# Dense products of a tick between the score and the transposes, in TensorE's order of work

## What is computed

```python
h = layernorm(x, gamma1, beta1)                      # layer 0
Q, K, V = h @ Wq + bq, h @ Wk + bk, h @ Wv + bv      # 16 heads of 16
attn = softmax(where(causal, Q K^T / 4, -inf))
x1 = x + (attn V) @ Wo + bo
x2 = x1 + gelu(layernorm(x1, ...) @ W1 + b1) @ W2 + b2
x  = x + gate * (x2 - x)
x  = layernorm(up(expert(gelu(down(x)))) + x)        # layer 1, expert of each sample
x  = layernorm(gelu(x @ Wi[e] + bi) @ Wo[e] + bo + x) # layer 2, expert of each sample
x  = layernorm(x) * (1 + scale) + shift              # layer 3
scores = Q K^T / 4 + attention_bias                  # (4, 16, 512, 512), masked
x = x + (softmax(scores) V) @ Wo + bo
x = x + gelu2(layernorm(x) * g2 + beta2 @ W1 + b1) @ W2 + b2
```

## Time and profile before

| | |
|---|---|
| three runs, median (lowest to highest) | 1131.92 us (1128.73 to 1132.33) |
| the profiled execution: its own time | 1131.03 us |
| its span, first to last instruction | 1128.9 us |
| PE busy | 997.0 us, 88% |
| DVE busy | 682.5 us, 60% |
| ACT busy | 685.0 us, 61% |
| POOL busy | 281.0 us, 25% |
| mean granted clock of PE, share of full speed | 0.982 |

### The profile page before, as it was taken

How to read it: one execution, slowest core, us unless ns; L and a number is a source line. 1 busy time by engine, 2 the same in 40 slices (tenths; PEclk the granted TensorE clock), 3 DMA queues, 4 the chain that set the end, 5 groups by cost and what they waited for, 6 DMA issues and landing times.

```text
span 1128.9 us, 22058 instructions
## 1 busy us (share of the span) xinstructions
PE 997.0 (88%) x7746; PEld 662.0 (59%) x7834; DVE 682.5 (60%) x1748; ACT 685.0 (61%) x1582; POOL 281.0 (25%) x473
## 2 busy tenths in 40 slices
PE   4878889898989899998889898899898999899868
PEld 2445556556546566566647466566575657657645
DVE  5668773645855747845772666746639754764740
ACT  3457565573765665776664746666657674675721
POOL 7310020000310640630120200730903370180010
PEclk9889999899999999999999999999999999999989
DMA  5879424206252454854625119667385486935400
GB/s 161 231 166 206 76 75 102 49 11 140 38 139 76 91 179 132 192 200 149 139 75 124 66 62 192 213 173 197 126 203 186 150 199 235 238 119 201 154 1 19
DMA packets 118351, 154.78 MB, mean 137 GB/s; under 512 B 12956, under 2 KB 80924, under 8 KB 118244
## 3 DMA queue, kind: packets, MB, share of 16 engines
q1 hardware_dynamic: 113636, 147.04, 48.8%
q0 software_dynamic: 1936, 3.97, 1.3%
q10 hardware_dynamic: 2672, 2.36, 0.6%
HBM read 134.47 MB, written 18.88 MB: 136 GB/s over the span
## 4 chain that ended last, share of the span: by engine, by line
PE 57%; ACT 16%; DVE 15%; issue 11%; DMA 0%; POOL 0%; DVEq 0%; ACTq 0%; POOLq 0%
PE bank L1384 15%; PE bank L1373 9%; PE bank L1480 8%; PE bank L1494 6%; PE bank L1335 6%; PE bank L1459 4%; ACT gT L933 3%; ACT bias L886 3%; DVE mrow L1216 3%; DVE bias L1225 3%; PE bank L1349 2%; PE bank L1359 2%; PE bank L1463 2%; ACT pT L894 2%; ACT L933 2%
## 5 line engine op out<-in xcount | busy, mean ns | idle before, releaser
L886 ACT ACTIVATE bias<-bias,mrow 128x512 f32<-128x512 f32 x256 | 184.1, 719 | 186.2 <-DVE mrow L1225 184.4
L1225 DVE CUSTOM_DVE_ANT_0 bias<-bank,bias 128x512 f32<-128x512 f32 x256 | 175.0, 687 | 199.1 <-PE bank L1459 88.0
L883 ACT ACTIVATE prob<-bank,mrow 128x128 f32<-128x128 f32 (+3 forms) x256 | 134.8, 527 | 191.7 <-DVE mrow L1216 189.7
L1216 DVE TENSOR_REDUCE mrow<-bank 128x1 f32<-128x128 f32 (+3 forms) x256 | 124.3, 487 | 172.4 <-PE bank L1465 171.0
L823 POOL TENSOR_TENSOR norm_rows_t<-norm_rows_t,minus_half 128x4 f32<-128x4 f32 x22 | 22.6, 1026 | 664.5 <-DVE norm_rows_t L1099 664.5
L1480 PE MATMUL bank<-ident,bias 128*128 128x128 f32 x1024 | 156.3, 275 | 33.4 <-ACT pT L894 24.3
L1480 PEld LDWEIGHTS bank<-ident,bias 128*128 128x128 f32 x1024 | 121.4, 141 | 106.7 <-ACT bias L886 53.5
L1373 PE MATMUL bank<-hT,w 128*128 128x512 f32 x384 | 181.2, 602 | 1.6 <-ACT hT L910 0.9
L1384 PE MATMUL bank<-w,gT 128*128 128x256 f32 x768 | 174.3, 381 | 0.0
L1459 PE MATMUL bank<-ks,qs 128*128 128x512 bf16 (+3 forms) x425 | 144.0, 339 | 30.3 <-ACT prob L883 28.2
L1233 DVE COPY pT<-bank 128x512 f32<-128x512 f32 (+3 forms) x263 | 150.9, 574 | 5.9 <-PE bank L1480 5.3
(11 more groups left out here) (165 smaller groups left out, 1128.0 us busy)
## 6 DMA issues: line engine op xcount, KB each, us to landing
bias<-in_fside_Bx16xSxS SPq DMA_DIRECT2D x128, 512.0 KB, 4.4
w<-in_L_cond_W SPq DMA_DIRECT2D x16, 1024.0 KB, 5.5
qs<-q_parts SPq DMA_DIRECT2D x30, 384.0 KB, 10.4
ks<-k_parts SPq DMA_DIRECT2D x30, 384.0 KB, 11.7
q_parts<-parts SPq DMA_DIRECT2D x80, 128.0 KB
k_parts<-parts SPq DMA_DIRECT2D x48, 128.0 KB
w<-in_L_cond_Wi SPq DMA_DIRECT2D x4, 1024.0 KB, 5.0
w<-in_L_cond_Wo SPq DMA_DIRECT2D x4, 1024.0 KB, 5.8
```

Source lines behind the costliest of these rows:

```text
L883: act.activation(prob_of(U), score_bank[U % 2][:, 0:n], ACT.Exp, bias=mrow[:, U % ROW_RING:U % ROW_RING + 1], accum_out=rsum[:, U % ROW_RI ...
L886: act.activation(prob_of(U), prob_of(U), ACT.Exp, scale=-1.0, bias=mrow[:, U % ROW_RING:U % ROW_RING + 1], accum_out=rsum[:, U % ROW_RING: ...
L1216: v.tensor_reduce(m, score_bank[U % 2][:, 0:n], AX_X, ALU.max, negate=True).then_inc(max_done, 1)
L1225: v.tensor_tensor_reduce(out=prob_of(U), in0=score_bank[U % 2][:], in1=prob_of(U), scale=-1.0, scalar=3e38, op0=ALU.add, op1=ALU.min, accu ...
```

## The change

In each tick, PE's dense steps now stand directly behind `scores(U)`, ahead of `turn(U - 2)`, `values` and `spread_sums`. Before, they stood behind all of these. No instruction is added or taken away, and no other engine's order changes.

```diff
                 if 0 <= U < ALL_UNITS:
                     scores(U)
+                for step, args in steps.get(U, []):
+                    do[step](*args)
                 V = U - TURN_LAG
                 if 0 <= V < ALL_UNITS:
                     turn(V)
@@
                 V = U - SPREAD_AT
                 if 0 <= V < ALL_UNITS and V % BATCH == 0:
                     spread_sums(V // BATCH)
-                for step, args in steps.get(U, []):
-                    do[step](*args)
```

## The result

The changed kernel takes **1140.23 us** (median of 5 runs, 1136.48 to 1143.42), the kernel before 1131.92 (5 runs, 1128.73 to 1132.42): ratio 1.0071, 95% interval 1.0051 to 1.0092. It is slower by 8.3 us, above the forecast's 1130 and above its range. The profiled execution of the changed kernel took 1136.62 us with a span of 1134.7, against 1131.03 and 1128.9: the two traces differ by only 5.6 us.

The account below looks back on a forecast made before the run. PE, busy 88% of the span, was taken as the bound, its waits all that order can win. Gains 15.6, losses 11.6 and 4.4, and 1.2 from sooner results gave 0.8 us won: 1130 us (1126 to 1134).

Parts of the forecast that it names:

- first `hidden`: First `hidden` of a feed-forward layer, 11 places beside attentions: product runs while the transpose would wait, 5.4 us won.
- `project`: First projection beside an attention: some places lose a transpose or wait about 0.5 us, one wins; 1.0 us lost.
- What bounds the kernel; the rule for gains and losses: PE busy 88% of the span; ready dense steps win the transposes' waits, waiting ones lose transposes and values put behind.
- `turn_tokens`, `turn_expert`, `up`: Steps waiting for operands lose 6.1, 2.9 and 1.6 us; two turns whose transposes waited win 1.0 us.
- Later causal `hidden` and `ff_out`: Causal dense products directly behind a score: taken as costing nothing, with 0.02 us either way per tick.
- The copy ahead of the maximum: VectorE's copy starts the maximum 0.26 us later in the mean; 45 waits hang on it, 4.4 us lost.
- Later biased `hidden`, `qk`, `down`: Fifth and ninth ticks of biased layers win 4.9 us, places beside `qk` 2.6, beside `down` 1.7.
- The waits of L1459 for probabilities stay: PE's scores waiting for probabilities from ScalarE: the change cannot move these waits, which stay near 28 us.
- The signs of being wrong: PE's summed waits move over 5 us; VectorE's score waits change more than the time; dense products take another time behind scores.
- Only the gains: Rival: lost transposes of waiting dense steps are won back one or two ticks on; 1120 us (1115 to 1126), chance 0.24.
- no effect: Rival: the new order does nothing, every wait turns up at the next transpose; 1131 us, chance 0.13.
- slower: Rival: VectorE's copy holds up maxima behind dense ticks, costing up to 10.5 us; 1136 us (1134 to 1142), chance 0.23.

Follow-up runs that it names:

- e5: Kernel before with only `hidden` and `ff_out` beside causal attentions moved directly behind the score: 1133.41 us, ratio 1.0023.
- e1: Kernel before with only `turn_tokens`, `turn_expert`, `up` and `project` moved directly behind the score: 1144.63 us, ratio 1.0111.
- e2: Kernel before with all dense steps except `turn_tokens`, `turn_expert`, `up` and `project` moved directly behind the score: 1124.75 us, ratio 0.9933.
- e9: Kernel before with only `turn_tokens`, `turn_expert`, `up` and `project` moved, to between transposes and values: 1134.48 us, ratio 1.0028.
- e10: Changed kernel with VectorE's copy behind the maximum only in causal ticks directly behind a dense tick: 1137.30 us, ratio 1.0057 to the kernel before.
- e8: Kernel before with only `qk`, `down` and `hidden` beside biased attentions moved directly behind the score: 1117.99 us, ratio 0.9882.
- e4: The changed kernel run again, unedited: 1138.32 us, ratio 1.0060 to the kernel before.

## Why the prediction was wrong, point by point

The mechanism was right and its sum was not. Three terms failed most: the gain of the first `hidden` (5.4 us forecast, 2.1 in the traces), the cost of `project` (1.0 forecast, 3.5), and a cost of the later causal steps that stood at nothing (3.5 in the traces, 2.6 measured in e5). With them a forecast gain of 0.8 us became a loss.

- **What bounds the kernel; the rule for gains and losses: right.** e1, e2 and e9 show the mechanism in its own quanta of 0.11 us a transpose and up to 1.0 a set of values, and e1 and e2 add up to the full change within their intervals.
- **`turn_tokens`, `turn_expert`, `up`: right in kind, a little small.** 5.1 + 2.9 + 1.6 = 9.6 us net in the sum, 11.6 in the traces, 0.7 of it lower clock.
- **First `hidden`, 5.4 us: oversized**, the largest error among the terms that the sum had. The shown place was right (0.58 forecast, 0.49 measured), and "the others give 0.2 to 0.7, one 1.2" was not: six biased places gave 1.8 us and five causal ones 0.3. The product gained against the transpose, but waits for hT there (L1373 in the waits above, 4.8 us; 0.9 before), and I took hT's time from the trace of before. Why some of these operands come later, place by place, was not taken apart.
- **`project`, 1.0 us: undersized**, 3.5 measured. I counted on the waits that the earlier trace rows show. Where the trace showed no wait, transposes and values had hidden one of up to 1.2 us, as in the rows of the projection above.
- **Later causal `hidden` and `ff_out`: a missing term**, 3.5 us in the traces, 2.6 in e5. Some 1.3 us of it is the pair product-behind-score (34 ticks by +0.05, seven by -0.05). I took nothing with 0.02 either way; it is 0.05 us in such a tick, outside that. The rest is the copy ahead of the maximum, in the Gelu ticks.
- **The copy ahead of the maximum, 4.4 us: about half as large.** e10's trace gives it 2.5 us, in ten ticks, and nothing in the others. The reason for taking it at 45 places by a mean of 0.26 us was wrong: of the copies that e10 moved, only those where a Gelu's chain hangs on the maximum gave anything back, six of them 0.33 us each.
- **Later biased `hidden`, `qk`, `down`: undersized.** 9.2 us forecast, 12.1 in the traces, and e8, which has the first biased `hidden` as well (1.8), won 13.7 us. Dense results coming sooner (1.2) may be part of it; that was not taken apart.
- **"The waits of L1459 for probabilities stay": right**, 30.8 us for 28.2.
- **The signs of being wrong.** Two of the three named ones came: VectorE's own waits for scores changed by 130 us, far more than the time, and a dense product took another time behind a score, by 0.05 us. The first says little, since that wait only moved to the copy. The remaining one, the sum of PE's waits, did not come: it moved by 1.5 us.
- **The sum.** Terms that were off by up to 3.5 us each, most to one side, make 7.1 us between -0.8 and the traces' +6.3. Of that 2.8 are the two stretches of lower clock, so the order itself stands at about +3.5, some 4 us above my sum. To the measured +8.3 (+7.2 in e4) 1 to 2 us more are missing beyond the traces, and they stand in the runs of the upper group. My sum and my range had no term for a meeting or for more time at the lower clock; whether these belong to the change is not shown.
- **The rivals.** *Only the gains* and *no effect* are refuted by e1 and e2. The *slower* one had the right sign and 1136, but not for its reason: the copy is 2.5 us of the loss, the waiting steps 15 (12.6 in e1).

## What to carry to other kernels

Each step of an in-order queue should be asked one question: is its operand there when the queue arrives? If it is, put it ahead of what waits; if not, put it behind everything that is ready, the next tick's first product too. One position for both kinds gives away what the other kind would win: the same edit applied to all steps was 0.7% slower, to the ready ones alone 1.2% faster, and with the waiting ones moved the other way 2.2% faster. A trace shows only the waits that are left; before moving a step forward, compute when its operand is done, since work with no wait behind it in the trace may be hiding one.

## What the runs showed of the hardware

- VectorE's L1128 (two instructions, 0.87 us) took 3.55 us beside GpSimd's L849, in one of two traces of the same kernel, and most of the 2.7 us went through to PE. The Trainium skill (SBUF — State Buffer, section SBUF: two separate sides) says that a VectorE operation with two SBUF inputs and a GpSimd operation that reads SBUF take one port pair as an exclusive lock, for a whole instruction, and that the loser stands still. L1128 has two such inputs, and by that the trace agrees in kind. But the rule has the one that starts first win, one instruction long: here the stall lasted over GpSimd's four products (2.55 us), though the second of the VectorE pair began at 387.89 us, 0.3 us before the first of them (388.20). Where VectorE's L1156 met the same four products elsewhere (at 730 us of the changed kernel's trace), the stall was short: two of L1156 took 1.98 us (0.69 for one alone) and the four products 3.46.
- A product directly behind the short causal mask product costs 0.05 us more from score to score than the same work with transposes in between, in 34 ticks, all but one of them the same in both traces that were walked for it (the changed kernel's and e5's). What causes it is open.
- A stretch of 3.4 us in which PE's granted clock was half cost 1.3 us in ticks 186 to 190 of the changed kernel's trace, and one cost 1.5 us in tick 216. Such stretches lie at other places in other traces of kernels with the same order of work.
- The time between two scores repeats to 0.01 us in most ticks, from execution to execution and from kernel to kernel. So two single traces resolve a change of 0.05 us in one tick, where the medians of five runs have intervals of some 2 us either way. The granted clock of both traces has to be read beside it.
